# A decoder layer on one core: the order of four small steps in each attention slot

## The reference, cut to what matters

```
q = rms_norm(h @ Wq + bq, gq);  k = rms_norm(h @ Wk + bk, gk);  v = h @ Wv + bv
attn = softmax(q k^T / sqrt(128));  out = attn v;  x = x + out @ Wo + bo
```

## Time and profile before

| | |
|---|---|
| time, median of 3 runs | 561.58 us (561.24 to 564.05) |
| profiled execution, first to last instruction | 560.2 us |
| PE busy | 530.3 us, 95% |
| DVE busy | 350.6 us, 63% |
| ACT busy | 355.9 us, 64% |
| POOL busy | 282.0 us, 50% |
| granted TensorE clock | 1.000 |

### The profile page before, as it was taken

One profiled execution on the slowest core, in us unless ns is written; L12 is line 12 of the kernel. 1 busy time (PEld: TensorE's weight loads), 2 busy tenths in 40 slices (PEclk: granted clock), 3 DMA queues, 4 the chain that ended last, 5 costly groups with the idle time before them and its releaser, 6 DMA issues.

```text
span 560.2 us, 10002 instructions
## 1 busy us (share of the span) xinstructions
PE 530.3 (95%) x3244; PEld 462.6 (83%) x3246; DVE 350.6 (63%) x695; ACT 355.9 (64%) x749; POOL 282.0 (50%) x237
## 2 busy tenths in 40 slices
PE   6999999899999999999999999999988888879887
PEld 5888888788888989999999999999967767767477
DVE  6222222495444677666666666666788888886755
ACT  3666666566666676767677777777655556556640
POOL 3444444545444454646464656555555545655340
PEclk9999999999999999999999999999999999999999
DMA  5333333223333212112111224414311111120002
GB/s 174 96 94 102 102 94 94 72 98 95 94 98 106 65 50 57 57 58 56 56 56 56 55 55 133 131 51 151 117 42 39 45 50 39 48 66 20 1 1 77
DMA packets 22775, 41.33 MB, mean 74 GB/s; under 512 B 3552, under 2 KB 3552, under 8 KB 22496
## 3 DMA queue, kind: packets, MB, share of 16 engines
q1 hardware_dynamic: 22752, 41.04, 25.2%
HBM read 39.98 MB, written 1.05 MB: 73 GB/s over the span
## 4 chain that ended last, share of the span: by engine, by line
PE 55%; DVE 19%; issue 10%; POOL 8%; ACT 6%; DMA 1%; POOLq 0%; SPq 0%; ACTq 0%; DVEq 0%
POOL acc_k L918 7%; PE acc L473 5%; PE acc L474 5%; PE acc L476 5%; PE p_v L545 4%; PE p_v L547 4%; PE p_v L546 4%; ACT probs L749 4%; PE acc L564 4%; PE acc L565 4%; PE acc L566 3%; PE p_t L531 3%; DVE nbias L1134 3%; DVE nmax L1132 2%; DVE ctx_f L1191 2%
## 5 line engine op out<-in xcount | busy, mean ns | idle before, releaser
L1082 DVE TENSOR_TENSOR w_lo<-raw,w_hi 128x512 fp32r<-128x512 f32 x64 | 44.2, 691 | 96.8 <-ACT w_hi L683 96.7
L749 ACT ACTIVATE probs<-p_s,nbias,rq_t 128x256 f32<-128x256 f32 x128 | 71.2, 561 | 51.6 <-DVE nbias L1134 51.6
L473 PE MATMUL acc<-xnt_hi,w_hi 128*128 128x512 f32 x256 | 100.3, 392 | 0.7 <-ACT xnt_hi L707 0.7
L474 PE MATMUL acc<-xnt_hi,w_lo 128*128 128x512 f32 x256 | 99.7, 390 | 0.0
L476 PE MATMUL acc<-xnt_lo,w_hi 128*128 128x512 f32 x252 | 98.2, 389 | 0.0
L936 POOL TENSOR_TENSOR wo_lo<-raw,wo_hi 128x512 fp32r<-128x512 f32 x31 | 40.1, 1293 | 100.2 <-ACT wo_hi L814 100.2
L683 ACT CAST w_hi<-raw 128x512 fp32r<-128x512 f32 x64 | 39.9, 623 | 67.8 <-PE acc L476 60.4
L545 PE MATMUL p_v<-w_hi,xnt_hi 128*128 128x256 f32 x256 | 77.3, 302 | 0.1
L547 PE MATMUL p_v<-w_hi,xnt_lo 128*128 128x256 f32 x256 | 72.4, 283 | 0.0
L546 PE MATMUL p_v<-w_lo,xnt_hi 128*128 128x256 f32 x256 | 72.3, 282 | 0.0
L918 POOL TENSOR_TENSOR acc_k<-acc_k,square 128x512 f32<-128x512 f32 x32 | 41.2, 1287 | 51.2 <-ACT square L698 51.2
(11 more groups left out here) (265 smaller groups left out, 1405.0 us busy)
## 6 DMA issues: line engine op xcount, KB each, us to landing
raw<-in_wv SPq DMA_DIRECT2D x36, 256.0 KB, 2.6
raw<-in_wk SPq DMA_DIRECT2D x32, 256.0 KB, 2.6
raw<-in_wq SPq DMA_DIRECT2D x32, 256.0 KB, 2.6
raw<-in_wo SPq DMA_DIRECT2D x31, 256.0 KB, 2.6
ctx_f<-in_ctx SPq DMA_DIRECT2D x2, 1024.0 KB, 6.0
xin<-in_x SPq DMA_DIRECT2D x4, 256.0 KB, 3.5
x_res<-in_x SPq DMA_DIRECT2D x4, 256.0 KB, 4.8
out_y<-xn SPq DMA_DIRECT2D x4, 256.0 KB, 2.1
```

Source lines behind the costliest of these rows:

```text
L473: pe.matmul(acc[n][:], hi[:, c, :], xnt_hi[:, c, :], start=(c == 0), stop=False)
L474: pe.matmul(acc[n][:], lo[:, c, :], xnt_hi[:, c, :], start=False, stop=False)
L749: act.activation(probs[:, b, a, :], p_s[:, a, :], ACT.Exp, bias=nbias[:, b, a:a + 1], scale=rq_t[:, 2 * b + a:2 * b + a + 1], accum_out=rs ...
```

## The change

Two engines do the same instructions in another order, in every slot of stage two. ScalarE makes `pt_hi` first and the K and Q parts of the next head behind it (in b = 0 slots; in b = 1 slots it has none to move). VectorE makes `pt_lo` ahead of `slot_max`. The special case of the very first slot (`q_hi` behind `pt_hi`) goes, since it is now the rule. No instruction is added or removed, and TensorE, GpSimd and SyncE keep their order.

```diff
                         act.activation(o_hi[:], p_o[:], ACT.Identity, bias=column(bv_c, h - 1)
                                        ).then_inc(o_hi_done, 1)
-                    if b == 0 and not (last and j == 2):
-                        act.wait_ge(scores_ready, 2 * h + 2)
-                        split_k_hi(h + 1)
-                        if not peeled(s, 0, 1):
-                            split_q_hi(h + 1)
                     if last and j == 3:
                         last_out_hi(0)
                     act.wait_ge(pt_ready, s + 1)
                     act.copy(pt_hi[:], p_t[:]).then_inc(pt_hi_done, 1)
-                    if peeled(s, 0, 1):
-                        split_q_hi(1)
+                    if b == 0 and not (last and j == 2):
+                        act.wait_ge(scores_ready, 2 * h + 2)
+                        split_k_hi(h + 1)
+                        split_q_hi(h + 1)
...
                     if b == 0 and not peeled(h, 0, 1):
                         out_lo(h - 1)
-                    if not end:
-                        slot_max(h + b, 1 - b)
                     if end:
                         last_out_lo(0)
                     dve.wait_ge(pt_hi_done, s + 1)
                     dve.tensor_tensor(pt_lo[:], p_t[:], pt_hi[:], ALU.subtract).then_inc(pt_lo_done, 1)
+                    if not end:
+                        slot_max(h + b, 1 - b)
```

## The result

The changed kernel takes **596.03 us** (595.62 to 597.0, 4 runs) against 562.31 us (561.24 to 564.05) for the kernel before on the same chip: 1.06 times, 95% interval 1.0576 to 1.0623. Forecast were 593 us and a range of 578 to 602.

What follows compares the result with a forecast made beforehand. TensorE was taken to bound the plain loop and VectorE the quantising stretch. 24 x 0.95 = 22.8 us plus 8 x 1.02 = 8.2 us gave +31.0 on 561.58, forecast 593 us, range 578 to 602.

Steps and rivals of the forecast that it cites:

- What bounds: TensorE bounds the plain loop, never waiting there; VectorE sets the quantising stretch's pace, where TensorE waits 12.0 us for `pt_lo`.
- First step, `q_lo` late: Plain loop, b = 0 slot: `q_lo` ends at 5.18 instead of 4.35, overspending 0.35 us of slack by 0.5 to 0.6.
- Second step, exponentials of b = 1 late: Plain loop, b = 1 slot: exponentials start at 3.54 instead of 1.84, a delay of 1.70 against 1.5 us of slack.
- The ring: Plain loop, dependency cycle from `k_lo` to the next head's `k_lo`: 10.35 instead of 9.40 us a head, +0.95.
- its sign, a wait before those transposes: Plain loop, b = 1 slots: TensorE idles before transposes, waiting for the divisions; transposes start at K + 3.44.
- Quantising stretch: Heads quantising the context, where VectorE sets the pace: 1.02 us more a head, x 8 = 8.2 us.
- the late entry: Start of the quantising stretch: a late entry could only add time; left out of the sum.
- The two parts: Quantising stretch: exponentials 0.66 later behind `pt_lo`, and +0.36 in the b = 0 slot with `nbias` held; 1.02 a head.
- The upper bound: Top of the range: 0.3 more per head in the ring makes the total +40, or 602 us.
- The holding of `nbias`: `nbias` ends with GpSimd's instruction; quantising stretch costs 8.2 us if held, 3.0 if not; held value taken.
- The much slower rival: Above 602 us: a division meets GpSimd's `w_lo` and is held some 1.3 us in every head; chance 0.06.
- The faster rival: Waits for `pt_lo` vanish and nothing replaces them: 561.58 - 12.0 = 550 us; chance 0.05.

Runs made afterwards that it cites:

- the run without K and Q chain: Changed kernel with `k_lo` and `q_lo` subtracted for 8 of 512 columns only; 583.1 us.
- the other `nbias`: Changed kernel with `nbias` made by two `tensor_scalar` operations of 128x1, one SBUF input each, instead of one `tensor_tensor`; 597.1 us.
- the fastest version: Kernel before, all three quantising steps moved ahead of the b = 1 divisions, `nbias` made by two one-SBUF-input `tensor_scalar` operations; 541.2 us.

## Why the prediction was right

- *What bounds* held: the loss sits where TensorE had been busy all the time, and the wait for `pt_lo` went without any gain. The forecast added 31.0 us; the medians are 33.7 apart.
- *First step, `q_lo` late:* the run without K and Q chain and the one with `pt_lo` first in b = 0 slots show it from both sides. Its own size was too small: 0.71 us a head (10.10) instead of 0.57.
- *Second step, exponentials of b = 1 late:* forecast 1.70 us later, measured 1.77 (3.61 instead of 1.84). Taken alone it costs 0.66 a head (10.05).
- *The ring:* forecast 10.35, measured 10.37 a head. One piece of its path is not the one that bound: the forecast went from the start K of `k_lo` through the held `nbias`, exponentials and divisions to the transposes at K + 3.44, and expected TensorE to wait there for the divisions. In the trace `q_lo` starts the scores and the transposes follow them (307.26, K + 3.48), 0.09 behind the divisions' end. The paths end together, which the forecast had said ("just before"), so the number holds; its sign, a wait before those transposes, did not show. The loop's 22.7 instead of 20.9: head 0, which I counted as an average one, lost 2.25 us (10.24 instead of 7.99 between its b = 0 transposes and the next head's; it has no output projection, so TensorE used to be through early), and the others lost 0.98 each instead of 0.95.
- *Quantising stretch:* 1.02 a head forecast, 0.88 measured (12.90). Two numbers were off: `k_lo` starts 0.70 and not 0.79 behind `k_hi` there (0.80 in the plain loop), and `pt_lo` to maximum takes 0.60 and not 0.66. The first head of the stretch cost 2.4 us, the late entry that the forecast had named and left out. The two parts can be told apart: with VectorE's old order in b = 1 slots a head takes 12.31, so `pt_lo` ahead of that maximum costs 0.59, and with the other `nbias` 12.61, 0.29 less. The sum came out at 8.6 for 8.2 because the errors cancel, which is luck.
- *The upper bound* does not follow as written: 0.3 more in each of the 24 heads of the ring gives 38 and 600 us; 602 takes it in all 32. The measured time is below both.
- *The holding of `nbias`* was priced as the rows had it, and `nbias` did end with `k_lo` and with `q_lo`. Of the two values weighed there, the trace chose the held one in the quantising stretch. In the plain loop the scores wait for `q_lo` with or without it.
- *The much slower rival* did not come here, but its mechanism is real: ScalarE's order alone calls it up. In the changed kernel the first division starts at 306.56, 0.24 behind the end of `q_lo`, and the second at 306.82, 0.09 ahead of `w_lo`; these narrow margins I had not counted.
- *The faster rival* fails as argued: the gaps for `pt_lo` (12.0 us) closed, the slack of what `pt_lo` was moved past ran out, and the kernel took 33.7 us more. The Trainium skill's advice (Perfetto Trace Analysis, "Optimization Strategy": within the regime of interest, find the gaps of the engine being optimized and make what they wait for start sooner or finish faster) leads to this rival if it is followed for these gaps alone.

What stays open: from which size on the form of `nbias` with one SBUF input would be held as well was not tried, nor whether ScalarE's order alone pays once the quantising steps and `nbias` are as in the fastest version, nor what the other `nbias` alone gives on the kernel before, where it is held for up to 1.11 us in a quantising head.

## What to carry to other kernels

Before moving an operation up in an in-order queue, write down for each operation that it passes how much slack its readers have; a step that is off the bounding engine costs nothing only until that slack is spent, and here 0.35 and 1.5 us were overspent by a few tenths, 24 times. When an engine's wait sits in one stretch only, ask what fills that stretch (here three elementwise steps on another engine) before reordering the loop that runs everywhere. And ask of each VectorE operation which GpSimd operation it will meet in its new place.

## What the runs showed of the hardware

- VectorE's divisions and quantising steps, `tensor_scalar` operations with one tensor input, are held by GpSimd as `nbias` is: 1.02 and 1.37 us instead of 0.35, 1.40 instead of 0.43. The Trainium skill (SBUF — State Buffer, "Who interferes with whom") lists `copy`, `cast` and `tensor_scalar` as able to enter modes that use two ports, and so to contend with GpSimd, where their operands meet certain conditions. The traces agree on the waiting; no run shows the ports. I had applied that section to `nbias` alone.
- A VectorE `tensor_tensor` of 128x2 with both inputs in SBUF waits for the end of a running GpSimd subtraction (0.47 to 1.15 us instead of 0.16 in the traces of both kernels, ending 0.01 to 0.03 behind it). The same product as `tensor_scalar` of 128x1 with a pointer scalar does not wait (0.20 to 0.21 in the middle of `k_lo`).
- The durations: a `tensor_scalar` of 128x512 float32 (L1194) took 0.43 us with GpSimd idle and 1.40 when it met a GpSimd operation; of 128x256 (L1143), 0.35 and up to 1.44. So of such an operation's recorded time a quarter to a third (0.35 of 1.44, 0.43 of 1.40) can be its own work, and the rest waiting: a busy share counts both.
- A VectorE operation that waits gets in between two GpSimd operations that follow each other at once: `nbias` between `k_lo` and `q_lo`. With two such operations in a row, each one waits for one of GpSimd's (ScalarE's order alone: 1.02 us with `q_lo`, 1.37 with `w_lo`).
- Two operations instead of one, both tiny, cost some 0.15 us on a ring (a slot of 5.06 instead of 4.91), even where each is short.
